# A two-layer decoder with top-32 attention: the steps that pick a head's 32 largest scores dealt out over the next head's pieces

## What is computed

```python
Q = (x_text @ Wq).reshape(1, 1024, 4, 32)           # 4 heads of width 32
K = (x_vision @ Wk).reshape(1, 6404, 4, 32)
scores = einsum('bthd,bghd->bhtg', Q, K) / sqrt(32)
topv, topi = jax.lax.top_k(scores, 32)              # per token and head
probs = softmax(topv)
attn = zeros_like(scores).at[..., topi].set(probs)
attn_mean = attn.mean(axis=1)                       # over the heads
c_t = einsum('btg,bgd->btd', attn_mean, x_vision @ Wv)
```

## Time and profile before

| | us |
|---|---|
| median of 3 runs (lowest, highest) | 1891.41 (1890.3, 1895.34) |
| the profiled execution | 1896.19 |
| its span, first to last instruction | 1894.4 |
| DVE busy | 1318.5 (70%) |
| PE busy | 1526.4 (81%) |
| ACT busy | 926.9 (49%) |
| POOL busy | 697.9 (37%) |

### The profile page before, as it was taken

The page is one execution under the profiler, slowest core; times in us unless marked ns, Lnnn a source line. Parts: engine busy times, 40 slices in busy tenths (PEclk is TensorE's granted clock), DMA queues, the critical chain, the costliest instruction groups (busy, mean ns, idle before and its releaser), DMA issues. The chain is left out here.

```text
span 1894.4 us, 20029 instructions
## 1 busy us (share of the span) xinstructions
PE 1526.4 (81%) x6681; PEld 814.2 (43%) x6737; DVE 1318.5 (70%) x3033; ACT 926.9 (49%) x1448; POOL 697.9 (37%) x526
## 2 busy tenths in 40 slices
PE   5776998999867468788878878887574399999798
PEld 2223443455435124455445545555453233333555
DVE  5997677565274599989999899898474646664233
ACT  5664114656213117777777777788211045554121
POOL 1765111121000008887888888788200200000012
PEclk8898999999878678998989898898777579999599
DMA  5000110000092200000000000000200200000000
GB/s 134 1 1 13 51 51 3 1 1 0 17 199 45 58 0 1 1 1 1 1 1 1 1 1 1 1 1 1 84 8 16 72 1 1 1 1 1 0 1 11
DMA packets 30244, 37.14 MB, mean 20 GB/s; under 512 B 13543, under 2 KB 23371, under 8 KB 29007
## 3 DMA queue, kind: packets, MB, share of 16 engines
q1 hardware_dynamic: 28586, 23.96, 4.6%
q10 hardware_dynamic: 1544, 11.79, 3.1%
HBM read 29.50 MB, written 6.24 MB: 19 GB/s over the span
## 5 line engine op out<-in xcount | busy, mean ns | idle before, releaser
L1472 PE MATMUL psum<-film_ka,film_context_qa 97*128 97x512 bf16 (+1 forms) x832 | 342.7, 413 | 145.7 <-DVE search_and_weigh_kept L1667 64.0
L1844 ACT ACTIVATE search_and_weigh_e<-psum,search_and_weigh_bias 128x512 f32<-128x512 f32 (+1 forms) x416 | 268.0, 666 | 111.2 <-PE psum L1474 107.3
L1667 DVE MAX8 search_and_weigh_kept<-psum 128x8 f32<-128x171 f32 (+2 forms) x1216 | 317.7, 324 | 5.0 <-PE psum L1474 3.8
L1474 PE MATMUL psum<-film_kb,film_context_qb 128*128 128x512 bf16 (+1 forms) x777 | 318.2, 410 | 0.0
L1693 DVE SCALAR_TENSOR_TENSOR search_and_weigh_e<-psum,film_context_top,search_and_weigh_e 128x512 f32<-128x512 f32 (+1 forms) x283 | 201.0, 717 | 37.5 <-ACT search_and_weigh_e L1844 35.1
L1715 POOL TENSOR_TENSOR search_and_weigh_e<-search_and_weigh_e,search_and_weigh_keep 128x512 f32<-128x512 f32 (+1 forms) x133 | 150.7, 1133 | 167.9 <-ACT search_and_weigh_keep L1823 165.0
L1472 PEld LDWEIGHTS psum<-film_ka,film_context_qa 97*128 97x128 bf16 x832 | 92.2, 111 | 253.4 <-DVE search_and_weigh_e L1693 99.2
L2678 DVE TENSOR_REDUCE gqa_attend_low<-psum 128x1 f32<-128x128 f32 (+7 forms) x128 | 96.6, 757 | 84.2 <-PE psum L2602 83.8
L2889 POOL TENSOR_TENSOR residual<-residual,top_expert_kept 128x1024 f32<-128x1024 f32 x8 | 18.7, 2344 | 357.1 <-DVE top_expert_kept L2862 357.1
L1749 PEld LDWEIGHTS psum<-ctx_rows,search_and_weigh_mean_T 128*128 128x128 f32 (+1 forms) x816 | 131.8, 207 | 32.8 <-issue 6.0
L1719 POOL TENSOR_TENSOR search_and_weigh_mean<-search_and_weigh_e 128x512 f32<-128x512 f32 (+1 forms) x104 | 134.1, 1290 | 12.3 <-DVE search_and_weigh_e L1693 5.1
(11 more groups left out here) (551 smaller groups left out, 2767.2 us busy)
## 6 DMA issues: line engine op xcount, KB each, us to landing
film_kb<-film_k_rows ACTq DMA_DIRECT2D x4, 1601.0 KB
film_ka<-film_k_rows ACTq DMA_DIRECT2D x3, 1601.0 KB
ctx_T<-in_ctx_T SPq DMA_DIRECT2D x1, 2401.5 KB
gqa_experts_w<-in_L_ffn_W SPq DMA_DIRECT2D x1, 2048.0 KB
film_convolve_back<-in_dft_back SPq DMA_DIRECT2D x1, 1728.0 KB, 13.1
film_k_rows<-cross_attention_film_hi SPq DMA_DIRECT2D x6, 256.0 KB, 2.0
film_k_rows<-cross_attention_film_mid SPq DMA_DIRECT2D x6, 256.0 KB, 2.0
film_k_rows<-cross_attention_film_low SPq DMA_DIRECT2D x6, 256.0 KB, 2.0
```

The costliest lines, as they stand in the source:

```text
L1472: pe.matmul(out, a["qa"][0:ROWS, h, rows], a["ka"][0:ROWS, h, c + b:c + b + cols], start=True, stop=False)
L1474: last = pe.matmul(out, a["qb"][:, h, rows], a["kb"][:, h, c + b:c + b + cols], start=False, stop=True)
L1667: last = dve.max(kept[:, h % 2, first + s, :], bank[:, lo:hi])
L1844: act.activation(e[:, n % RING, sub, 0:PIECES[u][1]], ps[:, SEARCH_BANKS + q % WEIGH_BANKS, 0:PIECES[u][1]], ACT.Exp, bias=bias[:, i % 2, ...
```

## The change

Three things. (1) `take_largest` is replaced by `pick(j, step)`, one of the eight steps of head j; steps 0 and 1 stand in the first piece after the head's last, 2 and 3 in the second, 4 and 5 in the third, 6 and 7 in the fourth. The even step stands behind the piece's first `max`, the odd step behind its last. Their order among themselves is kept by a semaphore of their own, `picked`, instead of a wait behind each. (2) `LAG` is 15. (3) The instruction for `flags` stands at the end of DVE's program of the part. DVE waits on `picked` before it overwrites a half of `kept` and before the limits. PE's, ACT's and POOL's programs are the same apart from `LAG`.

```diff
-    LAG = NCH + 1 if searching else 1
+    LAG = NCH + 2 if searching else 1
+    PICKS = 2 * TOP // 8
...
-        def take_largest(i, h):
-
-            j, k = i * NH + h, h % 2
+        def pick(j, step):
+
+            k = j % 2
             all_kept = kept[:, k, :, :].rearrange("p s e -> p (s e)")
-            link(dve.reduce_max(eighth[:, j:j + 1], kept[:, k, :, 7], AX))
-            for r in range(TOP // 8):
-                eight = a["top"][:, j, 8 * r:8 * r + 8]
-                link(dve.max(eight, all_kept))
-                if r < TOP // 8 - 1:
-                    link(dve.match_replace(all_kept, eight, all_kept, GONE))
-            if j == NT * NH - 1:
-                dve.tensor_tensor(a["flags"][:], eighth[:], a["top"][:, :, TOP - 1], ALU.is_gt).then_inc(flagged, 1)
+            if step == 0:
+                dve.wait_ge(searched, NCH * (j + 1))
+                dve.reduce_max(eighth[:, j:j + 1], kept[:, k, :, 7], AX).then_inc(picked, 1)
+                return
+            round_, replace = divmod(step - 1, 2)
+            eight = a["top"][:, j, 8 * round_:8 * round_ + 8]
+            dve.wait_ge(picked, PICKS * j + step)
+            if replace:
+                dve.match_replace(all_kept, eight, all_kept, GONE).then_inc(picked, 1)
+            else:
+                dve.max(eight, all_kept).then_inc(picked, 1)
...
                 r = NH * G + sub
+                head, after = r // NCH - 1, r % NCH
+                picking = searching and 0 <= head < NT * NH and after < PICKS // 2
                 if search_piece(r):
                     i, h, u = search_piece(r)
                     dve.wait_ge(search_done, r + 1)
+                    if u == 0 and i * NH + h >= 2:
+                        dve.wait_ge(picked, PICKS * (i * NH + h - 1))
...
                         last = dve.max(kept[:, h % 2, first + s, :], bank[:, lo:hi])
+                        if s == 0 and picking:
+                            pick(head, 2 * after)
                     last.then_inc(searched, 1)
-                    if u == NCH - 1:
-                        dve.wait_ge(searched, r + 1)
-                        take_largest(i, h)
+                elif picking:
+                    pick(head, 2 * after)
+                if picking:
+                    pick(head, 2 * after + 1)
...
                     if sub == 0:
+                        dve.wait_ge(picked, PICKS * NH * (i + 1)) if searching else None
...
         if searching:
+            dve.tensor_tensor(a["flags"][:], eighth[:], a["top"][:, :, TOP - 1], ALU.is_gt).then_inc(flagged, 1)
             dve.wait_ge(flagged, 1)
```

More of the change, by code:

```diff
@@ L1595, in weigh_program @@
     chain_act, keep_ready, summed_ready = m.sem("chain_act"), m.sem("keep_ready"), m.sem("summed_ready")
+    picked = m.sem("picked")
     search_done, searched, found, flagged, exp_done, summed, ln_done, bias_ready, least_ready, mask_ready = (
```

## The result

| | before | changed |
|---|---|---|
| median, us (lowest to highest) | 1891.8 (1890.3 to 1895.3) | 1831.3 (1829.6 to 1831.8) |
| profiled execution, us | 1896.2 | 1831.0 |
| its span, us | 1894.4 | 1829.2 |

The ratio is 0.9676 (95% interval 0.9659 to 0.9693): 60.5 us less, where 43 were forecast. Measured a second time (e9_after_again) it was 0.9678 (0.9663 to 0.9693). The time lies within the predicted range of 1825 to 1876, but outside the 1838 to 1860 of the forecast itself, and nearer to rival (a), 1827.

What follows compares the result with a forecast made beforehand. The prediction took DVE (VectorE) as the bound, the other engines not far behind. Overlap -32, head 31 -4, waits -10 and lag +3 summed to -43 us: 1848 us from 1891.4, forecast 1838 to 1860, range 1825 to 1876.

Steps and rivals of the forecast that it cites:

- rival (a): Combined search and weighting: DVE stays saturated, its 41.5 us of waits shrink to 11; -64 us, so 1827; chance 12%.
- The overlap: DVE's picking steps, dealt between independent maxima, each start 0.08 us early: 1.03 us less a head, -32 us for 31 heads.
- Rival (c): DVE's picking steps: no overlap, each costs its full length wherever it stands; -11 us, so 1880; chance 12%.
- The waits: DVE's 41.5 us of waits for other engines in the combined stretch: -10 us taken, from -30 to +12.
- rival (b): Combined stretch: POOL, PE and ACT become the bound, waits grow by 12 us; -21 us, so 1870; chance 18%.
- Head 31 and the lag: Last head's steps leave the path in weighting alone, -4 us; weighting one group later, +3 us.
- Rival (d): Dealt pieces: later bank release and masking make DVE wait in the next piece; +9 us, so 1900; chance 5%.
- no stop of PE above 2 us: Sign in the combined stretch: PE, which stood still for nearly 4 us at a run, never stops above 2 us.
- clock above 0.91: Sign in the combined stretch: PE's granted clock rises above 0.91.
- waits for ACT near 25: Sign: DVE's waits for ACT come to near 25 us instead of 33.
- 520 to 540 us combined: Sign: the 89 groups of search and weighting together take 520 to 540 us.
- weighting alone about 65: Sign: the stretch after the search, with weighting alone, takes about 65 us.

Runs made afterwards that it cites:

- e9_after_again: The changed kernel unchanged, timed once more on the same chip as two later kernels, against the kernel before: 1834.4 us, ratio 0.9678.
- e6_lag_warm: The kernel before with LAG 15 and PE computing each head's third search piece seven times, nothing dealt out: 1868.9 us, ratio 0.9860 to the kernel before.
- e2_behind: The changed kernel with a DVE wait right behind each picking step, so no successor starts early: 1863.2 us, ratio 0.9849 to the kernel before.
- e5_warm: The kernel before, lag 14, with PE computing each head's third search piece seven times while weighting goes on too: 1869.7 us against 1897.1, ratio 0.9869.
- e1_lag: The kernel before with LAG 15 and nothing else, the run of eight steps kept: 1910.4 us against 1892.7, ratio 1.0100.

## Why the prediction was right, and where it was off

Along the runs, each against the kernel before (ratio x 1892 us): the lag alone +19; with PE kept busy at the same lag -26, so 45 us hang on the stops and the clock; dealt out without overlap -29; dealt out with it -61. By the part's own time (ends and combined) the same ladder is **+16 (lag), -38 (PE's stops filled, the clock kept), -10 (dealt out instead of filled), -31 (overlap)**, together -63; the ratios give +19, -45, -2, -33, because the repeating kernel is also shorter behind the part. Of the -10, 7 us lie at the ends, where e6_lag_warm repeats nothing; in the combined stretch filling the stops and dealing them out come to nearly the same, 539.0 and 536.2 us, with clocks of 1.00 and 0.98. That the dealing works through the clock is inferred from this; no run deals out and holds the clock down.

The direction and the mechanism were right, the size was not: the result is in the range because the range was drawn to take in rival (a). Term by term:

- **The overlap**, forecast at -32 us: -32 (e2_behind to changed). The reading that independent neighbours start 0.08 us early carried over to replacements and value loads, of which no row had shown it. In search alone, a head takes 12.3 us instead of 13.8. Rival (c) falls. A wait behind 252 of the 256 steps cost 32 us, 0.13 us a step. The Trainium skill ("VectorE: DVE Perf Modes", "The DRAIN you can't avoid") reports from eight copies in a row that a semaphore behind each costs nothing extra. That doesn't carry over to this case, where each wait keeps an independent successor back. The section also says that a next instruction that is not held starts earlier, which the prediction left out; here the traced starts lie 0.08 to 0.09 us inside the forerunner.
- **The waits** were the term that was mis-sized. The prediction took -10 us of a possible -30: "PE no longer stands still for nearly 4 us and loses less clock" stood there as one of two reasons, without a price. The idle time before instructions that had to wait for another engine fell from 41.5 to 14 us, 27.5 us. That is 17.5 us more than the term had, and 17.5 us are what the forecast was short by. That the two agree so well is chance in part: by the rows, the overlap saved some 6 us more than forecast in the combined stretch, and small instructions lost some 6 us beside POOL (last section). The earlier trace rows held the key: the clock fell to 0.57 behind the run, so PE ran mostly at half its rate just when the lead had to be rebuilt, and 0.91 over the stretch is 0.09 x 2 x 576 = 104 us at 1.2 GHz. e5_warm prices it at 24 us of the part, at lag 14. The reason against, that everybody else has less time, shows no cost: POOL went to 91% and PE to 88% of the stretch, and rival (b) didn't come.
- **Rival (a)**, 1827, names what happened (waits shrinking to 11 us; 14 were measured), and had 12%.
- **Head 31 and the lag**, forecast at -4 and +3 us. Their share at the ends held: the overlap of the first four heads, the two groups more and head 31's run make -4.1 + 2.9 + 4.9 - 4 = -0.3 us by the prediction's own numbers, and the ends went from 121.2 to 120.8. In the kernel before, the same lag cost 18 us (e1_lag), 6 of them as a longer combined stretch where 6.4 less were expected. A sum of groups prices the lag only where PE doesn't stop.
- **Rival (d)**, DVE waiting at dealt steps, didn't happen: no idle time stands before any picking step.
- Of the signs named ahead: steps starting inside their forerunner, yes; 12.3 us a head of search alone (three heads in the 36.91 us from 655.85 to 692.76) where 12.8 were expected; no stop of PE above 2 us, yes (1.4); clock above 0.91, yes (0.99); waits for ACT near 25, no (8.0); 520 to 540 us combined, no (510); weighting alone about 65, yes: the 60 us before were counted to 1341, some 6 us behind the last addition, and so counted the stretch is now 66 us (the 61.3 of the rows above end at the flags).

## What to carry to other kernels

A run of dependent steps on the bounding engine costs twice here: each step starts behind its forerunner's end instead of inside it (a maximum takes 0.51 us to the next start instead of 0.37), and TensorE, which feeds it, stops for up to 3.8 us and comes back at a granted clock of 0.6 to 0.75. Deal such a run out between independent instructions, over more than two pieces (four and eight did about the same), and price the clock that a stop costs as a term of its own. A later start of the consumer was cheap only where nobody stopped; measure it alone before it is blamed or praised.

## What the runs showed that was not expected

A small DVE instruction with two inputs in SBUF that starts inside one of POOL's doesn't end before it. In the changed kernel, two of the three such instructions of a tile's limits in the first tile, before POOL has any work:

```profile
699.12 0.26 DVE L1689 TENSOR_TENSOR search_and_weigh_shifted<-film_context_top 128x128 f32<-128x128 f32 x1
...
701.69 0.14 DVE L1697 TENSOR_TENSOR search_and_weigh_bias<-search_and_weigh_total,film_context_top 128x4 f32<-128x4 f32 x1
```

and the first of them in the last tile, across POOL's instructions:

```profile
1217.07 1.16 POOL L1729 TENSOR_TENSOR search_and_weigh_e<-search_and_weigh_e,search_and_weigh_keep 128x512 f32<-128x512 f32 x1
...
1217.24 1.14 DVE L1689 TENSOR_TENSOR search_and_weigh_shifted<-film_context_top 128x128 f32<-128x128 f32 x1
...
1218.31 1.26 POOL L1733 TENSOR_TENSOR search_and_weigh_mean<-search_and_weigh_e 128x512 f32<-128x512 f32 x1
```

DVE's one starts inside POOL's and ends with it, at 1218.4 against 1218.2. The same holds for all 21 such instructions of the seven later tiles in the kernel before, and for 20 of 21 in the changed one: each starts while POOL is at work and ends 0.01 to 0.15 us behind POOL's instruction, or at its own full length where that is longer. The one exception, at 769.39, starts just ahead of POOL's and takes 0.27 us. So the effect isn't new, and how much it costs hangs on the moment. The bias started shortly before POOL's end in the kernel before and took 0.38 us on average; in the changed kernel it starts early in POOL's and takes 0.99 in the six later tiles of the combined stretch. With the first instruction (0.32 before, 0.77 now) some 1.1 us a tile are given back this way. No run took POOL's work away to show it.

The other surprise is e5_warm: useless matmuls in a stop made the kernel 1.3% faster, and the same number of them elsewhere made it 3.2% slower.
